# Merged attention and FFN kernel: a mask in two parts, LayerNorm's variance plus epsilon and negated mean on VectorE, and the last two steps in another order

## The chip, the cores and the metric

One NeuronCore of a Trainium2 chip runs the kernel. The metric is device time in microseconds of one execution. Three timed executions of the kernel before took 692.0, 689.85 and 688.17 us (median 689.85). A fourth one was recorded by the hardware profiler and took 687.63 us, of which the instructions span 685.6 us.

Engine names in the profile: PE is TensorE's matmuls, PEld its weight loads, DVE is VectorE, ACT is ScalarE, POOL is GpSimd, SP is SyncE (DMA queues).

## The reference

The input x is 8 x 1024 tokens of D = 256, in float32. An attention block without softmax is followed by two LayerNorms, then comes a gated FFN whose inputs and weights are rounded to a 4-bit grid in blocks of 16, and a third LayerNorm:

```
q, k, v = heads(x@Wq + bq), heads(x@Wk + bk), heads(x@Wv + bv)   # 16 heads of 16
q = elu(q) + 1;  k = elu(k) + 1;  k = k / sqrt(sum(k*k) + 1e-6)
y = x + ((q @ k^T) @ v) @ Wo + bo
y = (y - mean)/sqrt(var + 1e-6) * gamma + beta                 # LN1
x = layernorm(x + y)                                            # LN2, eps 1e-5
fp4(a): per block of 16: scale = max(max|a|/6, 1e-12); grid value nearest a/scale; times scale
h = silu(fp4(x) @ fp4(w_gate)^T) * (fp4(x) @ fp4(w_up)^T)       # inner width 704
out = layernorm(x + fp4(h) @ fp4(w_down)^T)                     # LN3, eps 1e-5
```

## The kernel before, in words

The 8192 tokens are T = 64 tiles of 128 tokens. The program is raw: each engine's instructions are written out in order by hand, and engines wait for each other by counting semaphores. Nothing reorders them. A first phase works through the projections of keys and values; it overlaps with the beginning of a merged loop `step(t)`, t from FIRST = -9 to LAST = T+5 = 69, which is a software pipeline over tiles. From t = 0 on one step does, on each engine and in this order:

- PE: gate and up matmuls of tile t (18, L477 to L479), the transposes of combined tile t+1 (L648), attention of tile t+9 (L618), and the down projection of tile t-4 (17 matmuls, L477 to L479, L670, L671). "Combined tile" n holds the 256 numbers of x of tile n and the 704 of h of tile n-4, 60 blocks of 16 to a token, as 15 lines of 64 numbers. They are quantised together.
- DVE: `residual` (L1129), the rounding mask `cut` of combined tile t+2 (L1098), block maxima of x (L1067), LN1's sum (L1135), statistics (L1157, L1160), the low part of h's codes `low_h` (L1112, which frees the bank into which PE transposes the next tile), the gating (L1121), statistics (L1167), `bn_aggr` of up to three LayerNorms (L1140), the low part of x (`low_x`, L1105, which PE's next gate and up matmuls wait for; in late steps it stands further back), the rest of the gating (L1123), block maxima of h (L1073), and `joint_scales` (L1086, L1088, L1090).
- POOL: `roots(t)`, four instructions on [128 x 3] for the three LayerNorms at once: variance + epsilon (L1287), negated mean (L1288), power -1/2 (L1290), negated mean times root (L1293); then the dequantisation of combined tile t+1 or t+2 (L1333, L1335, or L1324), the division by scales (L1302 for h, L1305 for x), and LN1's affine (L1311, L1315).
- ACT: evictions of transposes to their high parts (L829, L843, L846), silu, the three normalisations (`ln1_apply`, `ln2_apply`, `ln3_apply`, L866 to L880), and conversions in the quantisation (L805, L807, L814).

There are three kinds of steps. For even n from 12 to 54 (`by_dma(n)`, 22 tiles) the transposes of combined tile n are done by DMA rather than PE; the mask then writes 16 lines (1024 numbers, one line is padding) where it writes 15 otherwise (960). From t = 57 on, and before 6, dequantisation comes at another place in POOL's list. For n > 63 the combined tile holds only h (11 lines, 704 numbers). After t = 63 there are no more gate and up matmuls; the remaining steps drain the pipeline.

## Time and profile before

| | before |
| --- | --- |
| timed executions, us | 692.0, 689.85, 688.17 (median 689.85) |
| profiled execution, us | 687.63 |
| its span, us | 685.6 |
| mean granted TensorE clock | 0.997 |
| PE busy, us (share of the span) | 667.9 (97%) |
| PEld busy | 584.8 (85%) |
| POOL busy | 612.0 (89%) |
| DVE busy | 570.2 (83%) |
| ACT busy | 524.4 (76%) |
| chain that ended last | PE 69%, POOL 13%, issue 9%, DMA 3%, DVE 3%, ACT 2% |

The span is the time from the first to the last recorded instruction; 687.63 - 685.6 = 2.03 us of the execution lie around it. Busy times are of one engine and overlap with those of the others. The chain is the work that ended last, followed back from the last instruction; a share there says who was waited for, on an average over all stages.

### The profile page before, as it was taken

To read this page: it belongs to the slowest core of one execution; us is meant where nothing else is said; L and a number is where in the kernel's file an instruction comes from. 1 tells how busy PE (TensorE), PEld (TensorE's weight loads), DVE (VectorE), ACT (ScalarE), POOL (GpSimd) and SP (SyncE) were. 2 spreads that over 40 slices of the span, in tenths; PEclk is the share of its full clock that TensorE was granted. 3 is DMA by queue.
4 is the path that set the end of the run, shared out by engine and by line. 5 is a ranking of instruction groups with operands and counts; after the bars stand their busy time and mean duration, and the time that the engine had idled before them with its cause. 6 is when DMAs were issued, how large, how long until landed. Compare 5 with 4: busy or idle time off the path is not lost.

```text
span 685.6 us, 14440 instructions
## 1 busy us (share of the span) xinstructions
PE 667.9 (97%) x4216; PEld 584.8 (85%) x4216; DVE 570.2 (83%) x1438; ACT 524.4 (76%) x1037; POOL 612.0 (89%) x925
## 2 busy tenths in 40 slices
PE   7999999999999899999999999999999999999995
PEld 6888888888887789888989998999989989999994
DVE  5678778776779888899899999999988899988774
ACT  4677777775778667788888889888898888887663
POOL 3988898998979998898999999999999999998766
PEclk9999999999999999999999999999999999999998
DMA  8543344444311111444757555665557664500001
GB/s 271 193 139 132 120 134 130 139 139 154 124 63 32 34 60 47 95 96 97 143 116 160 129 128 115 124 163 131 126 98 119 112 145 95 110 17 16 32 17 46
DMA packets 51099, 74.39 MB, mean 109 GB/s; under 512 B 26380, under 2 KB 31054, under 8 KB 51022
## 3 DMA queue, kind: packets, MB, share of 16 engines
q1 hardware_dynamic: 50602, 73.35, 42.8%
q8 instruction: 34, 0.56, 0.3%
q14 instruction: 43, 0.35, 0.2%
q10 hardware_dynamic: 420, 0.13, 0.1%
HBM read 41.75 MB, written 25.89 MB: 99 GB/s over the span
## 4 chain that ended last, share of the span: by engine, by line
PE 69%; POOL 13%; issue 9%; DMA 3%; DVE 3%; ACT 2%; SPq 0%; POOLq 0%; DVEq 0%; ACTq 0%
PE banks L477 18%; PE banks L478 17%; PE banks L479 17%; PE banks L618 6%; POOL arena L1335 4%; PE banks L648 3%; POOL arena L1302 3%; PE banks L540 3%; DMA resid<-scales_scratch 2%; PE banks L488 2%; POOL arena L1305 1%; POOL lnbuf L1311 1%; PE banks L501 1%; POOL arena L1324 1%; DMA resid<-in_L_attn_Wv_dram 1%
## 5 line engine op out<-in xcount | busy, mean ns | idle before, releaser
L477 PE MATMUL banks<-wgu_hi,actT_lo 128*128 128x512 f32 (+1 forms) x384 | 145.5, 379 | 0.3 <-DVE actT_lo L1105 0.2
L478 PE MATMUL banks<-wgu_lo,actT_hi 128*128 128x512 f32 (+1 forms) x384 | 143.6, 374 | 0.0
L479 PE MATMUL banks<-wgu_hi,actT_hi 128*128 128x512 f32 (+1 forms) x384 | 143.2, 373 | 0.0
L477 PE MATMUL banks<-wd_hi,actT_lo 128*128 128x256 f32 x320 | 100.3, 313 | 0.1
L1302 POOL TENSOR_TENSOR arena<-arena 128x704 f32<-128x704 f32 x64 | 89.6, 1401 | 10.8 <-DVE arena L1090 10.8
L479 PE MATMUL banks<-wd_hi,actT_hi 128*128 128x256 f32 x320 | 90.3, 282 | 0.0
L478 PE MATMUL banks<-wd_lo,actT_hi 128*128 128x256 f32 x320 | 90.2, 282 | 0.0
L477 PEld LDWEIGHTS banks<-wgu_hi,actT_lo 128*128 128x128 f32 x384 | 72.4, 188 | 11.9 <-DVE actT_lo L1105 1.5
L479 PEld LDWEIGHTS banks<-wgu_hi,actT_hi 128*128 128x128 f32 x384 | 72.1, 188 | 10.5
L478 PEld LDWEIGHTS banks<-wgu_lo,actT_hi 128*128 128x128 f32 x384 | 72.4, 189 | 9.6
L1335 POOL TENSOR_TENSOR arena<-arena,s 128x960 f32<-128x960 f16 (+2 forms) x46 | 75.9, 1649 | 0.0
L807 ACT ACTIVATE arena<-arena 128x960 f16<-128x960 bf16 (+2 forms) x68 | 64.8, 953 | 5.9 <-POOL arena L1305 5.2
L1290 POOL TENSOR_TENSOR rstd<-ve,mhalf 128x3 f32<-128x3 f32 x78 | 68.9, 883 | 0.0
L1112 DVE TENSOR_TENSOR actT_lo<-banks,actT_hi 128x768 fp32r<-128x768 f32 x64 | 60.6, 947 | 9.7 <-ACT actT_hi L846 9.7
L814 ACT ACTIVATE arena<-arena 128x1024 uint16<-128x1024 uint16 (+3 forms) x68 | 66.3, 975 | 2.2
L1260 POOL TENSOR_TENSOR xs<-arena 128x512 f32<-128x512 f32 x48 | 61.0, 1293 | 7.0 <-DMA arena<-in_L_attn_beta_dram 7.0
L618 PE MATMUL banks<-mo,resid 128*128 128x256 f32 x256 | 65.8, 380 | 0.0
L859 ACT ACTIVATE arena<-banks 128x512 f32<-128x512 f32 x64 | 37.8, 591 | 32.4 <-PE banks L479 32.4
L477 PEld LDWEIGHTS banks<-wd_hi,actT_lo 128*128 128x128 f32 x320 | 60.8, 190 | 1.6 <-DVE actT_lo L1112 0.3
L478 PEld LDWEIGHTS banks<-wd_lo,actT_hi 128*128 128x128 f32 x320 | 60.9, 190 | 1.3
L479 PEld LDWEIGHTS banks<-wd_hi,actT_hi 128*128 128x128 f32 x320 | 60.8, 190 | 0.0
L1073 DVE TENSOR_REDUCE arena<-arena 128x44 f32<-128x704 f32 x64 | 56.8, 887 | 2.5
(146 smaller groups left out, 1966.3 us busy)
## 6 DMA issues: line engine op xcount, KB each, us to landing
xs<-x_plus_scratch SPq DMA_DIRECT2D x32, 512.0 KB, 4.2
x_plus_scratch<-xs SPq DMA_DIRECT2D x24, 512.0 KB, 2.9
resid<-scales_scratch SPq DMA_DIRECT2D x22, 512.0 KB
arena<-in_L_attn_x_dram SPq DMA_DIRECT2D x32, 256.0 KB, 3.6
out_dram<-arena SPq DMA_DIRECT2D x32, 256.0 KB, 6.1
x_plus_scratch<-arena SPq DMA_DIRECT2D x4, 512.0 KB, 2.9
x_plus_scratch<-resid SPq DMA_DIRECT2D x4, 512.0 KB, 3.4
resid<-in_L_attn_x_dram SPq DMA_DIRECT2D x4, 256.0 KB, 6.2
```

What stands on the lines that cost most here:

```text
L477: nc.tensor.matmul(dst, sl, mh, start=(k == 0), stop=False, skip_group_check=shared)
L478: nc.tensor.matmul(dst, sh, ml, start=False, stop=False, skip_group_check=shared)
L479: last = nc.tensor.matmul(dst, sh, mh, start=False, stop=(ended and k == n - 1), skip_group_check=shared)
L618: last = nc.tensor.matmul(ps[:, at_bank(u), 0:D], resid[:, u, m * P:(m + 1) * P], mo[:, u // TPB, m, :], start=(m == 0), stop=(m == KT - 1))
L807: nc.scalar.activation(vqb[n % 2][:, a // RW:b // RW, 0:RW].bitcast(F16), lines(halves(vy[:, n % 2, a:b])), ACT.Copy, scale=F16_ONE).then_ ...
L814: nc.scalar.activation(q, q, ACT.Copy, bias=ROUND_HALF).then_inc(half_s, 1)
L1073: nc.vector.tensor_reduce(am[:, n % 2, XR:RN, 0:4], h[:, n % 2, :].rearrange("p (r c e) -> p r c e", c=4, e=BLK), AX.X, ALU.max, apply_abs ...
L1112: nc.vector.tensor_tensor(vT_lo[:, n % 2, XC:VC, :], v_ps[:, XC:VC, :], f32(vT_hi[:, n % 2, XC:VC, :]), ALU.subtract).then_inc(h_lo_s, 1)
L1260: nc.gpsimd.tensor_tensor(to[:, :, kind, :], xin[:, 2 * r:2 * r + 2, :], row[:, :].unsqueeze(1).broadcast_to([P, 2, D]), ALU.add).then_inc ...
L1290: nc.gpsimd.tensor_tensor(rstd[:, s, :], ve[:, :], mhalf[:, :].broadcast_to([P, 3]), ALU.pow).then_inc(pow_s, 1)
L1302: last = nc.gpsimd.tensor_tensor(blocks(vy[:, s, D:VW]), blocks(h[:, s, :]), each(inv[:, s, D // BLK:VB]), ALU.mult)
L1335: nc.gpsimd.tensor_tensor(blocks(va[:, (n + 1) % 2, a:b]), blocks(vqc[n % 2].bitcast(F16)[:, a:b]), each(s14[:, n % 4, a // BLK:b // BLK]) ...
```

## The change

1. `cut(n)`, the rounding mask on DVE: for the 22 tiles that are turned by DMA, the one instruction on 16 lines becomes two, on lines 13 to 15 and 0 to 12 (`SPLIT = 13`).
2. A new DVE function `root_sums(t)` stands behind the last `bn_aggr` of a step and makes variance + epsilon (a tensor_tensor) and the negated mean (a tensor_scalar), both [128 x 3], in buffers of two slots. It does so for t from 2 to LAST; POOL's `roots(t)` then waits for these two and does only the power and the product. For t below 2 POOL still does all four. `roots(70)`, which nothing used, is gone.
3. In the last steps: `cut(66)` moves on DVE from step 64 to step 63, between the maxima of h and `joint_scales(67)`; on POOL `dequantise(66)` moves ahead of `over_scales(67)`; on ACT `ln3_apply` stands behind the eviction of h's high part from t = 64 on.

```diff
+        SPLIT = 13
+        sums_s = sem("sums_by_dve")
+        SUMMED = [*range(2, LAST + 1)]
+        def summed(t):
+            return 2 * len([u for u in SUMMED if u <= t])
...
-                if there(t - 6):
+                if there(t - 6) and t < T:
                     ln3_apply(t - 6, t)
                 if there(t + 1) and not late(t):
                     high_x(t + 1)
                 if there(t + 1 - LAG) and h_with_x(t + 1):
                     high_h(t + 1)
+                if there(t - 6) and t >= T:
+                    ln3_apply(t - 6, t)
...
                 if by_dma(n):
-                    b = VC * P
-                nc.vector.tensor_scalar(lines(vqc[n % 2].bitcast(U16)[:, a:b]), vqb[n % 2][:, a // RW:b // RW, 0:RW],
-                                        ROUND_MASK, None, ALU.bitwise_and).then_inc(round_s, 1)
+                    nc.vector.tensor_scalar(out[:, SPLIT:, :], source[:, SPLIT:VC * P // RW, 0:RW], ROUND_MASK, None,
+                                            ALU.bitwise_and)
+                    b = SPLIT
+                nc.vector.tensor_scalar(out[:, a // RW:b, :], source[:, a // RW:b, 0:RW], ROUND_MASK, None,
+                                        ALU.bitwise_and).then_inc(round_s, 1)
...
+            def root_sums(t):
+                s = t % 2
+                dve.wait_ge(agg_s, aggregated(t - 1))
+                after(dve, root_s, rooted(t - 2))
+                nc.vector.tensor_tensor(ve_dve[:, s, :], mv[:, s, :, 1], eps_v[:, :], ALU.add).then_inc(sums_s, 1)
+                nc.vector.tensor_scalar(nm_dve[:, s, :], mv[:, s, :, 0], -1.0, None, ALU.mult).then_inc(sums_s, 1)
...
-                if joint(t + 2):
+                if joint(t + 2) and t != T:
                     cut(t + 2)
...
+                if t + 1 in SUMMED:
+                    root_sums(t + 1)
                 if there(t + 1) and t >= 0 and not late(t):
                     low_x(t + 1)
...
+                if t + 1 == T:
+                    cut(t + 3)
                 if joint(t + 4) and not pair(t + 33):
                     joint_scales(t + 4)
...
-                nc.gpsimd.tensor_tensor(ve[:, :], mv[:, s, :, 1], eps_v[:, :], ALU.add).then_inc(ve_s, 1)
-                nc.gpsimd.tensor_tensor(nm[:, :], mv[:, s, :, 0], mone[:, :].broadcast_to([P, 3]), ALU.mult).then_inc(nm_s, 1)
-                pool.wait_ge(ve_s, rooted(t))
-                nc.gpsimd.tensor_tensor(rstd[:, s, :], ve[:, :], mhalf[:, :].broadcast_to([P, 3]), ALU.pow).then_inc(pow_s, 1)
+                if t in SUMMED:
+                    pool.wait_ge(sums_s, summed(t))
+                    sums, means = ve_dve[:, s, :], nm_dve[:, s, :]
+                else:
...
+                nc.gpsimd.tensor_tensor(rstd[:, s, :], sums, mhalf[:, :].broadcast_to([P, 3]), ALU.pow).then_inc(pow_s, 1)
...
+                if t == T:
+                    dequantise(t + 2)
                 if joint(t + 3):
                     over_scales(t + 3)
                 if there(t + 7):
                     ln1_affine(t + 7)
-                if joint(t + 2) and not SHIFT <= t < UNSHIFT:
+                if joint(t + 2) and not SHIFT <= t < UNSHIFT and t != T:
                     dequantise(t + 2)
```

How the instructions stand now, first on DVE in an even step whose tile t+2 is turned by DMA, from its first instruction to the second part of the gating. Before (the mask is L1098, the aggregates L1140, the gating's second part L1123):

```order
L1129 TENSOR_TENSOR arena<-banks,resid 128x256
L1098 TENSOR_SCALAR arena<-arena 128x1024
L1067 TENSOR_REDUCE arena<-resid 128x4x4
L1135 TENSOR_TENSOR lnbuf<-banks,xs 128x256
L1157 BN_STATS st<-arena 128x6
L1160 BN_STATS st<-lnbuf 128x6
L1112 TENSOR_TENSOR actT_lo<-banks,actT_hi 128x768
L1121 TENSOR_TENSOR arena<-arena,banks 128x512
L1167 BN_STATS st<-lnbuf 128x6
L1140 BN_AGGR mv<-st 128x2 x3
L1123 TENSOR_TENSOR arena<-arena,banks 128x192
```

The same place after (line numbers are those of the changed kernel: the masks are L1113 and L1116, the new sums L1164 and L1165). The rows between the maxima of x and the first part of the gating are as before and left out by starting a second piece:

```order
L1147 TENSOR_TENSOR arena<-banks,resid 128x256
L1113 TENSOR_SCALAR arena<-arena 128x192
L1116 TENSOR_SCALAR arena<-arena 128x832
L1080 TENSOR_REDUCE arena<-resid 128x4x4
L1153 TENSOR_TENSOR lnbuf<-banks,xs 128x256
L1182 BN_STATS st<-arena 128x6
```

```order
L1139 TENSOR_TENSOR arena<-arena,banks 128x512
L1192 BN_STATS st<-lnbuf 128x6
L1158 BN_AGGR mv<-st 128x2 x3
L1164 TENSOR_TENSOR ve_dve<-mv,eps_v 128x3
L1165 TENSOR_SCALAR nm_dve<-mv 128x3
L1141 TENSOR_TENSOR arena<-arena,banks 128x192
```

The mask has become two instructions, and two instructions on 3 numbers stand between the aggregates and the gating's second part.

Next, DVE from the maxima of h in step 63 to `low_h` in step 64. Before (the scales of tile 67 are L1086 to L1090, the mask of tile 66 is L1098):

```order
L1073 TENSOR_REDUCE arena<-arena 128x11x4
L1086 TENSOR_SCALAR arena<-arena 128x44
L1088 TENSOR_SCALAR s<-arena 128x44
L1090 RECIPROCAL arena<-arena 128x44
L1129 TENSOR_TENSOR arena<-banks,resid 128x256
L1098 TENSOR_SCALAR arena<-arena 128x704
L1157 BN_STATS st<-arena 128x6
L1140 BN_AGGR mv<-st 128x2
L1112 TENSOR_TENSOR actT_lo<-banks,actT_hi 128x768
```

After (the mask is L1116, the scales L1099 to L1103, the sums L1164 and L1165, `low_h` L1130):

```order
L1086 TENSOR_REDUCE arena<-arena 128x11x4
L1116 TENSOR_SCALAR arena<-arena 128x704
L1099 TENSOR_SCALAR arena<-arena 128x44
L1101 TENSOR_SCALAR s<-arena 128x44
L1103 RECIPROCAL arena<-arena 128x44
L1147 TENSOR_TENSOR arena<-banks,resid 128x256
L1182 BN_STATS st<-arena 128x6
L1158 BN_AGGR mv<-st 128x2
L1164 TENSOR_TENSOR ve_dve<-mv,eps_v 128x3
L1165 TENSOR_SCALAR nm_dve<-mv 128x3
L1130 TENSOR_TENSOR actT_lo<-banks,actT_hi 128x768
```

The mask has moved ahead of the scales, and the sums stand ahead of `low_h`.

Last, POOL from step 64 to the roots of step 65. Before (L1302 divides tile 67 by its scales, L1333 and L1335 dequantise tile 66):

```order
L1302 TENSOR_TENSOR arena<-arena 128x704
L1333 TENSOR_TENSOR arena<-arena,s 128x64
L1335 TENSOR_TENSOR arena<-arena,s 128x704
L1287 TENSOR_TENSOR ve<-mv,eps_v 128x3
L1288 TENSOR_TENSOR nm<-mv,mone 128x3
L1290 TENSOR_TENSOR rstd<-ve,mhalf 128x3
L1293 TENSOR_TENSOR nmr<-nm,rstd 128x3
```

After (L1369 and L1371 dequantise tile 66, L1338 divides tile 67, L1327 is the power and L1329 the product):

```order
L1369 TENSOR_TENSOR arena<-arena,s 128x64
L1371 TENSOR_TENSOR arena<-arena,s 128x704
L1338 TENSOR_TENSOR arena<-arena 128x704
L1327 TENSOR_TENSOR rstd<-ve_dve,mhalf 128x3
L1329 TENSOR_TENSOR nmr<-nm_dve,rstd 128x3
```

The dequantisation stands ahead of the division, and two of the four instructions of the roots are gone.

## Rows read from the trace of the kernel before

**Rows 1.** Stretches: span, then each engine's busy us (instructions), PE clock, DMA share, GB/s
```profile
core 0: us, PE busy (x) PEld busy (x) DVE busy (x) ACT busy (x) POOL busy (x), PEclk, DMA share, GB/s
...
208.00:248.00 40.00, 37.19 (x199) 31.28 (x196) 35.29 (x101) 28.83 (x52) 38.20 (x63) 1.00 0.13 40
...
279.00:318.00 39.00, 37.60 (x226) 33.52 (x225) 35.51 (x92) 30.91 (x60) 32.99 (x48) 1.00 0.55 113
318.00:577.00 259.00, 258.78 (x1563) 234.39 (x1563) 237.42 (x655) 222.95 (x431) 248.88 (x341) 1.00 0.61 124
...
664.00:685.60 21.60, 13.20 (x106) 12.42 (x104) 11.13 (x26) 10.04 (x19) 14.56 (x34) 0.92 0.10 37
```

**Rows 2.** Groups by form, POOL: line, out<-in, xcount | busy us, mean ns | idle before
```profile
L1287 POOL TENSOR_TENSOR ve<-mv,eps_v 128x3 f32<-128x3 f32 x78 | 18.3, 235 | 5.9 <-DVE mv L1140 5.6 <-POOL nmr L1293 0.2
L1288 POOL TENSOR_TENSOR nm<-mv,mone 128x3 f32<-128x3 f32 x78 | 15.5, 199 | 0.0
```

**Rows 3.** Groups by form, the masks on DVE
```profile
L1098 DVE TENSOR_SCALAR arena<-arena 128x960 uint16<-128x960 uint16 x38 | 24.4, 642 | 0.2 <-ACT arena L814 0.2
L1098 DVE TENSOR_SCALAR arena<-arena 128x1024 uint16<-128x1024 uint16 x22 | 12.8, 581 | 2.4 <-ACT arena L814 2.4
```

**Rows 4.** Timeline at 294 and 383: start us, us, instruction, [idle before <-releaser]
```profile
294.44 1.79 POOL L1335 TENSOR_TENSOR arena<-arena,s 128x960 f32<-128x960 f16 x1
294.47 2.04 DVE L1098 TENSOR_SCALAR arena<-arena 128x1024 uint16<-128x1024 uint16 x1
298.83 1.07 PE L648 MATMUL banks<-ident,arena 128*128 128x128 f32 x8 [0.94 <-DVE actT_lo L1112]
...
383.05 0.43 DVE L1098 TENSOR_SCALAR arena<-arena 128x1024 uint16<-128x1024 uint16 x1 [0.23 <-ACT arena L814]
```

**Rows 5.** Timeline at 403, a DVE instruction with two SBUF inputs
```profile
402.84 0.75 POOL L1315 TENSOR_TENSOR lnbuf<-lnbuf,xs 128x256 f32<-128x256 f32 x1
403.16 0.97 DVE L1002 TENSOR_TENSOR resid<-resid 128x512 f32<-128x512 f32 x1
```

**Rows 6.** Timeline at 118, two small DVE instructions beside two of POOL's
```profile
118.02 2.54 POOL L1260 TENSOR_TENSOR xs<-arena 128x512 f32<-128x512 f32 x2
118.78 0.55 DVE L942 TENSOR_SCALAR lnbuf<-lnbuf 128x24 f32<-128x24 f32 x1
119.24 0.16 DVE L943 TENSOR_SCALAR lnbuf<-lnbuf 128x24 f32<-128x24 f32 x1
```

**Rows 7.** Timeline, aggregates and what POOL runs, first and last of 36 steps
```profile
321.56 0.30 DVE L1140 BATCH_NORM_AGGREGATE mv<-st 128x2 f32<-128x6 f32 x3
321.90 0.74 POOL L1311 TENSOR_TENSOR lnbuf<-lnbuf,gamma_b 128x256 f32<-128x256 f32 x1
...
573.63 0.30 DVE L1140 BATCH_NORM_AGGREGATE mv<-st 128x2 f32<-128x6 f32 x3
573.97 0.63 POOL L1305 TENSOR_TENSOR arena<-resid,arena 128x256 f32<-128x256 f32 x1
```

**Rows 8.** Timeline at 650, step 61
```profile
649.90 1.79 POOL L1335 TENSOR_TENSOR arena<-arena,s 128x960 f32<-128x960 f16 x1
649.96 0.17 DVE L1140 BATCH_NORM_AGGREGATE mv<-st 128x2 f32<-128x6 f32 x1
650.59 0.42 DVE L1105 TENSOR_TENSOR actT_lo<-banks,actT_hi 128x256 fp32r<-128x256 f32 x1 [0.45 <-ACT actT_hi L829]
```

**Rows 9.** Timeline from 667, steps 64 and 65
```profile
667.42 1.40 POOL L1302 TENSOR_TENSOR arena<-arena 128x704 f32<-128x704 f32 x1 [1.34 <-DVE arena L1090]
667.53 0.51 DVE L1098 TENSOR_SCALAR arena<-arena 128x704 uint16<-128x704 uint16 x1
668.58 0.93 DVE L1112 TENSOR_TENSOR actT_lo<-banks,actT_hi 128x768 fp32r<-128x768 f32 x1
670.34 0.20 POOL L1287 TENSOR_TENSOR ve<-mv,eps_v 128x3 f32<-128x3 f32 x1
670.44 0.88 PE L648 MATMUL banks<-ident,arena 128*128 128x128 f32 x6 [1.32 <-POOL arena L1335]
670.65 0.85 POOL L1290 TENSOR_TENSOR rstd<-ve,mhalf 128x3 f32<-128x3 f32 x1
```

More of the change, by code:

```diff
@@ L93, in build @@
         ve, nm = (sb(n, [P, 3]) for n in ("ve", "nm"))
+        ve_dve, nm_dve = (sb(n, [P, 2, 3]) for n in ("ve_dve", "nm_dve"))
         rstd, nmr = (sb(n, [P, 2, 3]) for n in ("rstd", "nmr"))
@@ L1095, in cut @@
                 after(dve, deq_s, n - 1)
+                source, out = vqb[n % 2], lines(vqc[n % 2].bitcast(U16)[:, 0:VC * P])
+                b = b // RW
                 if by_dma(n):
-                    b = VC * P
-                nc.vector.tensor_scalar(lines(vqc[n % 2].bitcast(U16)[:, a:b]), vqb[n % 2][:, a // RW:b // RW, 0:RW],
-                                        ROUND_MASK, None, ALU.bitwise_and).then_inc(round_s, 1)
+                    nc.vector.tensor_scalar(out[:, SPLIT:, :], source[:, SPLIT:VC * P // RW, 0:RW], ROUND_MASK, None,
[3 more added lines that the diff above has]
+                                        ALU.bitwise_and).then_inc(round_s, 1)
             def low_x(n):
@@ L1278, in roots @@
             def roots(t):
-                if t < FIRST + 2:
+                if t < FIRST + 2 or t > LAST:
                     return
                 s = t % 2
-                pool.wait_ge(agg_s, aggregated(t - 1))
+                if t not in SUMMED:
+                    pool.wait_ge(agg_s, aggregated(t - 1))
                 after(pool, z1_s, min(t + 6, T))
@@ L1286, in roots @@
                 after(pool, root_s, rooted(t - 1))
-                nc.gpsimd.tensor_tensor(ve[:, :], mv[:, s, :, 1], eps_v[:, :], ALU.add).then_inc(ve_s, 1)
-                nc.gpsimd.tensor_tensor(nm[:, :], mv[:, s, :, 0], mone[:, :].broadcast_to([P, 3]), ALU.mult).then_inc(nm_s, 1)
-                pool.wait_ge(ve_s, rooted(t))
-                nc.gpsimd.tensor_tensor(rstd[:, s, :], ve[:, :], mhalf[:, :].broadcast_to([P, 3]), ALU.pow).then_inc(pow_s, 1)
+                if t in SUMMED:
+                    pool.wait_ge(sums_s, summed(t))
+                    sums, means = ve_dve[:, s, :], nm_dve[:, s, :]
+                else:
+                    sums, means = ve[:, :], nm[:, :]
+                    by_pool = rooted(t) - summed(t) // 2
+                    nc.gpsimd.tensor_tensor(sums, mv[:, s, :, 1], eps_v[:, :], ALU.add).then_inc(ve_s, 1)
+                    nc.gpsimd.tensor_tensor(means, mv[:, s, :, 0], mone[:, :].broadcast_to([P, 3]), ALU.mult).then_inc(nm_s, 1)
+                    pool.wait_ge(ve_s, by_pool)
+                    pool.wait_ge(nm_s, by_pool)
+                nc.gpsimd.tensor_tensor(rstd[:, s, :], sums, mhalf[:, :].broadcast_to([P, 3]), ALU.pow).then_inc(pow_s, 1)
                 pool.wait_ge(pow_s, rooted(t))
-                pool.wait_ge(nm_s, rooted(t))
-                nc.gpsimd.tensor_tensor(nmr[:, s, :], nm[:, :], rstd[:, s, :], ALU.mult).then_inc(root_s, 1)
+                nc.gpsimd.tensor_tensor(nmr[:, s, :], means, rstd[:, s, :], ALU.mult).then_inc(root_s, 1)
             def over_scales(n):
```

## The prediction

> **What bounds the kernel now.** I read the table of stretches first, then the groups by form for the instructions that the change touches, then the timelines at the places where one of them stands next to a running POOL instruction. In the table [rows 1] the reader is to compare PE's busy time with the length of the stretch. From 318 to 577 us PE works 258.78 of 259.00 us: 0.22 us is all that any change of DVE or POOL can gain there, over 36 steps. Gaps are left in three other stretches: 2.81 us at 208 to 248 (40.00 - 37.19), 1.40 us at 279 to 318, and 8.40 us in the last 21.60, where the pipeline drains. POOL's share of the page (89%) is therefore no bound by itself. The second thing to see is how little the other engines have in hand beside a full PE: DVE works 237.42 of the 259.00 us, so it idles 21.58 us, 0.60 us a step; POOL idles 10.12 us, 0.28 a step. A change that moves work from POOL to DVE gains nothing while PE is full, and loses once DVE gets over 0.60 us a step.
>
> The third reading is what the two engines do to each other. A DVE instruction with two SBUF inputs that started at 403.16 lasted 0.97 us and ended at 404.13; POOL's L1315 had ended at 403.59, 0.54 before, which leaves 0.54 for the work on its 512 numbers [rows 5]. The mask of 16 lines at 294.47 lasted 2.04 us instead of 0.43: it ended at 296.51, and POOL's L1335, started 0.03 before it, at 296.23 [rows 4]. At 118.78 a small DVE instruction lasted 0.55 us, ending 0.04 after the end of POOL's first L1260 (118.02 + 1.27); the next, at 119.24, took 0.16, though POOL's second L1260 was under way [rows 6]. I read this as: certain DVE instructions wait until POOL's running instruction ends, and one that stands right behind can slip into the same gap.
>
> **The change, part by part.** The sum is made against the profiled execution, 687.63 us (span 685.6, and 2.03 around it).
>
> *POOL's two instructions.* 78 of 235 ns and 78 of 199 ns [rows 2]; pipelined, they take 0.31 us a step (L1287 starts at 670.34, L1290 at 670.65) [rows 9]. 67 to 68 of the 78 steps lose them, some 21 us of POOL's busy time. While PE is full this is worth at most the 0.22 us of idle PE, and I take 0.2.
>
> *Steps 1 to 5, 208 to 248.* POOL saves 0.31 in each of four steps, 1.24 us together. But the new sums stand directly ahead of `low_x`, which PE's next gate and up matmuls wait for, and there the sums' own 0.23 and their wait (both below) come in. The ends are -1.2 (all of POOL's gain arrives at PE) and +1.1 (four waits of 0.28 do). I take 0, the middle.
>
> *The mask in two parts.* 22 instructions took 581 ns on the mean [rows 3]; an undisturbed one took 0.43 [rows 4]. 22 x 0.15 us, 3.3 us, is hence what POOL's running instruction held them up by. Three of them fall on L1335, at steps 10 to 14; the one of 2.04 us is shown, and behind it PE stood 0.94 us for `low_h` [rows 4]. The 15-line form, with an odd count, takes 642 ns, but has no hold-up to speak of in its mean [rows 3]; 11 lines take 0.51 [rows 9]. So 13 lines should take about 0.57, between those two. Three lines have no row; the nearest is a small instruction of 0.16 [rows 6], and I take 0.23 for 192 numbers. With the overlap of neighbours the pair is about 0.73, 0.30 more than an undisturbed 0.43, on every second step: 0.15 us of DVE per step. In return no mask waits for L1335. The gain is PE's idle time at 279 to 318, -1.4, if all of it is due to them; the other end is 0, if the pair is held up as well.
>
> *The new sums.* Two small instructions issue in 0.23 us (the nearest: 0.16 for one [rows 6], less the overlap of the two). Variance + epsilon has two SBUF inputs, so by the reading above it waits for what POOL runs. Step by step over 318 to 577 I compared the end of the last aggregate with POOL's instruction at that time. In the first of the 36 steps the aggregates end at 321.86 and the next POOL instruction starts at 321.90; in the last they end at 573.93 and L1305 starts at 573.97 [rows 7]. Both starts lie 0.04 behind the aggregates, so the sum either just slips ahead or waits out most of 0.63 to 0.74. Over the 36 steps the remaining time of POOL's instruction was 0.10 to 0.67 us, 0.28 on the mean. So a step gets 0.15 (mask) + 0.23 + 0.28 = 0.66 us more on DVE, against 0.60 of idle time. 36 x 0.06 = 2.2 us, of which I take +2.0. The ends: 0 if the sums do not wait (0.38 fits in 0.60), and 36 x 0.66 = 24 us if none of DVE's idle time can be used. Idle time is usable as far as DVE waits in it for PE, and most of it does (`residual` waits for the down projection), so the value near 0 is the better one. What is late next, when it overflows, is `low_h` and with it PE's transposes.
>
> What is queued behind the wait: on DVE the gating's second part, the maxima of h and the scales; for the scales waits POOL's division (L1302). On POOL the power now waits for the sums in place of the aggregates, later by 0.23 to 0.51 a step, against the 0.31 which it saves; that comes out near nothing.
>
> *Step 61.* Here dequantisation stands in another place, and L1335 starts at 649.90, 0.23 before the aggregate ends (649.96 + 0.17). The sums stand still until 651.69. `low_x`, which ran at 650.59 [rows 8], would start at about 651.73: 1.14 us later, in a stretch without slack behind it.
>
> *Steps 64 and 65.* Now L1302 starts at 667.42, L1335 ends at 670.38, and PE, idle for 1.32 us, transposes tile 66 at 670.44 [rows 9]. Moved ahead of L1302's 1.40 us, the dequantisation no longer sets this. Next comes `low_h`, which ended at 669.51 (668.58 + 0.93): 0.93 us are to be had. But L1302 then starts shortly ahead of step 64's sums, and about 0.85 us of it are left when they come. So `low_h` would start at 668.58 + 1.14 (step 61) + 0.85 + 0.23 (the sums) = 670.80 and end at 671.73: PE starts 1.3 later than at 670.44, and with a last 0.1 for the steps behind I take +1.4. The ends: -0.9 if the sums never wait, and +2.8 if they wait for the whole of L1335 and L1302 (1.79 + 1.40 + twice 0.23, less those 0.93, rounded up). That ACT's `ln3_apply` stands further back has its price in these ends.
>
> The sum: 0 - 1.4 (masks) - 0.2 (POOL late) + 2.0 (DVE over its idle time) + 1.4 (end) = +1.8 us, so 687.63 + 1.8 = 689.4 for an execution like the profiled one. The four known times average 689.4 (692.0, 689.85, 688.17, 687.63), 1.8 above the profiled one; with this the forecast is 691.2 us.
>
> **The rivals.**
>
> *A. The sums do not wait for POOL.* For it: POOL's small instructions and DVE's aggregates run side by side in [rows 7] with no hold-up, and three numbers may be too few to conflict. Against it: the small one at 118.78 [rows 6]. Then 0.38 us a step hide in 0.60, step 61 costs nothing, the end gains 0.9, the masks 1.4, POOL 0.2, and of the 1.2 in steps 1 to 5 half arrives: -3.1, so 686.3.
>
> *B. DVE becomes the bound.* The negated mean, on one input, does not slip through behind the sum but waits for POOL's next instruction as well. A step then gets some 0.65 us more (L1305 takes 0.63, L1311 0.74 [rows 7]): 1.31 against 0.60, from 0.60 on everything counts, 36 x 0.71 = 25.6, less 1.6 for masks and POOL, plus 1.4 at the end. That is slower, 714.8; where only every second step is caught, 702. Against it: the second of two small ones did slip through [rows 6]. The Trainium skill, page "Advanced Engine Details and Errata", section "VectorE Performance Modes", speaks for it: an instruction from SBUF to SBUF takes the second port, which it shares with GpSimd so that they block each other, where the major counts of source and destination are both even, or odd, above 1 and equal. Three and three would be such a case, so by that page the negated mean waits by itself. The mask of 16 lines fits the even half of this rule [rows 4]; a mask of 15 lines, odd and equal on both sides, should then be held up too, and its mean of 642 ns shows no such waits [rows 3], so the rows do not bear out the odd half.
>
> *C. Everything hides.* The waits fit into DVE's idle time and the gains are where PE does not wait: no change, 689.4.
>
> **How the numbers follow.** Forecast 0.43, A 0.30, B 0.17, C 0.10. The forecast's own range is 688 to 695 (early steps and masks at their good or bad end, steady steps at +0 to +4). From A I take the upper part, so the range begins at 685.5; B's mild part reaches 698. Less than 1 in 10 is left out on either side. A measurement of this kernel can tell about 0.5% from no change, 3.45 us: faster means under 686.0, slower over 692.9. Faster: two thirds of A and a little of the forecast, 0.22. Slower: B with 0.16 and the upper third of the forecast with 0.15, 0.31. The same: 0.47.
>
> **What would show it.** The sum behind the aggregates lasting 0.1 to 0.7 us and ending with a POOL instruction: right; 0.16 throughout: A. The negated mean above 0.3 us: B. Masks of 13 lines at about 0.57 and none above 1 us at steps 10 to 14; PE gaps at 279 to 318 below 0.5. PE at 258.8 of 259 again in the steady steps would make +2.0 wrong; a longer stretch with PE waiting for `low_h` or `low_x` would bear it out. In step 61 the sums should last 1.4 to 1.8 us. PE's transposes of tile 66 should start near 672, later than before by over 1 us, released by DVE and not by POOL; earlier than 670.44 would make the step on the end wrong.

## The result and the profile after

The changed kernel is slower: 702.38 us (median of 6 runs) against 689.01, a ratio of 1.0191 with a 95% interval of 1.0164 to 1.0218. One of the six runs of the kernel before took 945.59 us; it is in that median and not in the ratio, and the other five have a median of 688.17. The forecast of 691.2 and its range up to 698.0 missed it. The profiled execution took 700.78 us, with a span of 698.7, 13.1 more than before.

PE's work is the same, 4216 matmuls at a mean granted clock of 0.996 (0.997 before), but its busy time rose from 667.9 to 675.5 us. So PE's idle time in the table below shows only part of the delay. DVE's busy time rose from 570.2 to 614.0 us, POOL's fell from 612.0 to 585.9. So DVE took on 43.8 us where POOL gave up 26.1. Where the end came later is read from the table of stretches. Its columns are those of [rows 1]; this is the changed kernel.

```profile
208.00:248.00 40.00, 36.36 (x198) 30.22 (x199) 38.09 (x107) 28.13 (x53) 37.98 (x54) 1.00 0.12 40
279.00:318.00 39.00, 38.93 (x241) 35.32 (x240) 36.44 (x109) 32.65 (x62) 32.43 (x40) 1.00 0.61 112
318.00:577.00 259.00, 256.42 (x1528) 229.78 (x1527) 253.82 (x730) 217.81 (x422) 228.89 (x264) 1.00 0.59 122
577.00:664.00 87.00, 83.88 (x520) 75.64 (x519) 79.85 (x205) 62.84 (x118) 70.31 (x84) 1.00 0.23 53
664.00:698.70 34.70, 24.31 (x164) 22.52 (x162) 25.63 (x63) 16.48 (x31) 17.83 (x25) 0.93 0.08 31
```

The kernel before, in the one of these stretches that [rows 1] leaves out:

```profile
577.00:664.00 87.00, 87.00 (x544) 79.42 (x543) 73.33 (x188) 65.47 (x121) 75.33 (x111) 1.00 0.18 48
```

At 279 to 318 PE is now full (38.93 of 39.00, before 37.60): the masks' part came as forecast. At 318 to 577 DVE works 253.82 of 259.00 us where it worked 237.42 [rows 1], and PE, which had waited 0.22 us, waits 2.58. At 577 to 664, where PE had been busy for the whole 87.00, it waits 3.12.

Time is best followed by when PE begins each step's gate and up matmuls. The changed kernel's beginning less that of before, in us, over the steps: 

```
step     0      6      10     15     50     57     60     63     end
       +1.34  +1.69  +1.64  -0.07  +5.00  +5.31  +8.33  +9.85  +13.12
```

The first 1.34 lie ahead of any changed instruction on the path; in the profiled executions below this number is between -0.4 and +1.5, so I put it down to the execution. From step 10 to 15 the kernel gains 1.7. It loses 5.1 from step 15 to 50, 4.5 from 57 to 63, and 3.3 in the drain.

The groups by form show the loss on DVE (line, tiles, shapes, count, then busy us and mean ns, then idle before). The two sums are L1164 and L1165, the masks' parts L1113 and L1116; [rows 3] has the mask in one.

```profile
L1164 DVE TENSOR_TENSOR ve_dve<-mv,eps_v 128x3 f32<-128x3 f32 x68 | 29.8, 438 | 2.6 <-DVE mv L1158 0.2
L1165 DVE TENSOR_SCALAR nm_dve<-mv 128x3 f32<-128x3 f32 x68 | 23.7, 348 | 0.1
L1116 DVE TENSOR_SCALAR arena<-arena 128x832 uint16<-128x832 uint16 x22 | 12.7, 577 | 0.0
L1113 DVE TENSOR_SCALAR arena<-arena 128x192 uint16<-128x192 uint16 x22 | 5.4, 244 | 1.3 <-ACT arena L824 1.3
```

The masks cost what was forecast (0.577 and 0.244 us, forecast 0.57 and 0.23). Both sums are long: 438 and 348 ns for three numbers, where an undisturbed one takes 0.15 to 0.16. The timeline of DVE shows how. First two steps, at 329 and 373 us (start, duration, instruction); what POOL runs there follows.

```profile
328.72 0.61 DVE L1164 TENSOR_TENSOR ve_dve<-mv,eps_v 128x3 f32<-128x3 f32 x1
329.26 0.15 DVE L1165 TENSOR_SCALAR nm_dve<-mv 128x3 f32<-128x3 f32 x1
...
373.46 0.16 DVE L1164 TENSOR_TENSOR ve_dve<-mv,eps_v 128x3 f32<-128x3 f32 x1
373.54 0.71 DVE L1165 TENSOR_SCALAR nm_dve<-mv 128x3 f32<-128x3 f32 x1
```

```profile
328.59 0.73 POOL L1347 TENSOR_TENSOR lnbuf<-lnbuf,gamma_b 128x256 f32<-128x256 f32 x1
...
372.69 0.73 POOL L1347 TENSOR_TENSOR lnbuf<-lnbuf,gamma_b 128x256 f32<-128x256 f32 x1
373.50 0.73 POOL L1351 TENSOR_TENSOR lnbuf<-lnbuf,xs 128x256 f32<-128x256 f32 x1
374.42 0.86 POOL L1327 TENSOR_TENSOR rstd<-ve_dve,mhalf 128x3 f32<-128x3 f32 x1 [0.19 <-DVE nm_dve L1165]
```

At 328.72 the sum starts 0.13 behind POOL's L1347 and lasts until 329.33, 0.01 past the end of L1347; the mean behind it takes 0.15. At 373.46 POOL's L1347 has just ended (373.42); the sum goes through at once, and the mean, started 0.04 after L1351, lasts to 374.25, 0.02 after L1351's end. POOL's power then has to wait for the mean. So one of the two is held in nearly every step: if the first finds the gap between two POOL instructions, the second does not, and is held for a whole one. Of the 36 steps from 15 to 50 the sum is held in 23, the mean in 12 (in one step both), neither in 2 (held means here: it lasts more than 0.2 us).

In the later steps POOL's instruction is L1371, 1.79 us long. DVE and POOL at step 58 (637 us) of the changed kernel, in that order:

```profile
637.32 0.16 DVE L1164 TENSOR_TENSOR ve_dve<-mv,eps_v 128x3 f32<-128x3 f32 x1
637.40 1.78 DVE L1165 TENSOR_SCALAR nm_dve<-mv 128x3 f32<-128x3 f32 x1
639.10 0.41 DVE L1123 TENSOR_TENSOR actT_lo<-banks,actT_hi 128x256 fp32r<-128x256 f32 x1
```

```profile
637.37 1.79 POOL L1371 TENSOR_TENSOR arena<-arena,s 128x960 f32<-128x960 f16 x1
```

`low_x` (L1123), which PE's next gate and up matmuls need, stands right behind. Step 59 repeats this, and in steps 57, 61, 62 and 63 the sum is held, for 1.79, 1.61, 1.31 and 1.32 us as its duration. Step 61 of [rows 8] and the drain of [rows 9] now read as follows (POOL's dequantisation L1371 and division L1338, DVE's sums and `low_h` L1130, PE's transposes L658, each engine by itself):

```profile
660.18 1.61 DVE L1164 TENSOR_TENSOR ve_dve<-mv,eps_v 128x3 f32<-128x3 f32 x1
661.71 0.15 DVE L1165 TENSOR_SCALAR nm_dve<-mv 128x3 f32<-128x3 f32 x1
661.78 0.41 DVE L1123 TENSOR_TENSOR actT_lo<-banks,actT_hi 128x256 fp32r<-128x256 f32 x1
...
675.25 1.32 DVE L1164 TENSOR_TENSOR ve_dve<-mv,eps_v 128x3 f32<-128x3 f32 x1
...
680.87 1.36 DVE L1165 TENSOR_SCALAR nm_dve<-mv 128x3 f32<-128x3 f32 x1
682.15 0.94 DVE L1130 TENSOR_TENSOR actT_lo<-banks,actT_hi 128x768 fp32r<-128x768 f32 x1
```

```profile
659.98 1.79 POOL L1371 TENSOR_TENSOR arena<-arena,s 128x960 f32<-128x960 f16 x1
...
675.19 1.36 POOL L1371 TENSOR_TENSOR arena<-arena,s 128x704 f32<-128x704 f16 x1
679.50 1.36 POOL L1371 TENSOR_TENSOR arena<-arena,s 128x704 f32<-128x704 f16 x1
680.82 1.40 POOL L1338 TENSOR_TENSOR arena<-arena 128x704 f32<-128x704 f32 x1
```

```profile
672.53 0.81 PE L658 MATMUL banks<-ident,arena 128*128 128x128 f32 x6
677.65 0.85 PE L658 MATMUL banks<-ident,arena 128*128 128x128 f32 x6 [1.21 <-DVE actT_lo L1130]
683.24 1.36 PE L658 MATMUL banks<-ident,arena 128*128 128x128 f32 x6 [2.71 <-DVE actT_lo L1130]
```

The transposes of tile 66 are the last of these rows: at 683.24, released by DVE, where they stood at 670.44, released by POOL [rows 9]. Of these 12.80 us, 9.85 were there when step 63 began.

### The profile page after: what moved, and what is told of

It is laid out like the page before. It is cut to its first block and busy times, and to the rows that moved or that the text cites. A ratio compares the mean times of both kernels' runs of the same rounds, so it can differ in the third digit from the quotient of the medians.

```text
span 698.7 us, 14455 instructions
## 1 busy us (share of the span) xinstructions
PE 675.5 (97%) x4216; PEld 587.9 (84%) x4216; DVE 614.0 (88%) x1596; ACT 523.5 (75%) x1037; POOL 585.9 (84%) x785
## 5 line engine op out<-in xcount | busy, mean ns | idle before, releaser
L487 PE MATMUL banks<-wgu_hi,actT_lo 128*128 128x512 f32 (+1 forms) x384 | 147.0, 383 | 5.5 <-DVE actT_lo L1123 5.3
L1338 POOL TENSOR_TENSOR arena<-arena 128x704 f32<-128x704 f32 x64 | 89.3, 1395 | 18.0 <-DVE arena L1103 14.8
L1371 POOL TENSOR_TENSOR arena<-arena,s 128x960 f32<-128x960 f16 (+2 forms) x46 | 76.5, 1662 | 0.0
L1360 POOL TENSOR_TENSOR arena<-wo_sb,resid 128x1024 f32<-128x1024 f16 x22 | 48.4, 2199 | 30.7 <-DMA wo_sb<-arena 30.7
L1327 POOL TENSOR_TENSOR rstd<-ve_dve,mhalf 128x3 f32<-128x3 f32 x68 | 58.4, 859 | 11.5 <-DVE nm_dve L1165 11.5
L1130 DVE TENSOR_TENSOR actT_lo<-banks,actT_hi 128x768 fp32r<-128x768 f32 x64 | 60.4, 943 | 6.4 <-ACT actT_hi L856 6.4
```

The costliest lines, as they stand in the source:

```text
L487: nc.tensor.matmul(dst, sl, mh, start=(k == 0), stop=False, skip_group_check=shared)
L1130: nc.vector.tensor_tensor(vT_lo[:, n % 2, XC:VC, :], v_ps[:, XC:VC, :], f32(vT_hi[:, n % 2, XC:VC, :]), ALU.subtract).then_inc(h_lo_s, 1)
L1327: nc.gpsimd.tensor_tensor(rstd[:, s, :], sums, mhalf[:, :].broadcast_to([P, 3]), ALU.pow).then_inc(pow_s, 1)
L1338: last = nc.gpsimd.tensor_tensor(blocks(vy[:, s, D:VW]), blocks(h[:, s, :]), each(inv[:, s, D // BLK:VB]), ALU.mult)
L1360: nc.gpsimd.tensor_tensor(v_turned(n)[:, a:VC, :], codes[:, a:VC, :].bitcast(F16), s_each[:, a:VC, :], ALU.mult).then_inc(deq_s, 1)
L1371: nc.gpsimd.tensor_tensor(blocks(va[:, (n + 1) % 2, a:b]), blocks(vqc[n % 2].bitcast(F16)[:, a:b]), each(s14[:, n % 4, a // BLK:b // BLK]) ...
```

## The experiments

The theory after the result (theory 1): each of the two sums, when it starts while POOL works on certain instructions, waits for that instruction's end; one right behind another can use the same gap. Rival 2: the loss comes from the masks or from the last steps' order. Rival 3: it comes from the longer way from aggregates over DVE to POOL's power. All ratios are to the kernel before, run on the same chip beside them: its median was 689.38 beside the first four, 689.13 beside the next four and 688.08 beside the last two.

| kernel | us | ratio (95%) |
| --- | --- | --- |
| all but the sums | 689.60 | 0.9999 (0.9977 to 1.0020) |
| the sums alone | 712.41 | 1.0336 (1.0295 to 1.0377) |
| changed, mean free of POOL | 694.64 | 1.0077 (1.0050 to 1.0105) |
| changed, mean and sum free | 687.39 | 0.9968 (0.9951 to 0.9985) |
| the same, masks in one | 690.81 | 1.0018 (0.9995 to 1.0041) |
| mean and sum free, masks of 15 lines | 688.35 | 0.9991 (0.9975 to 1.0007) |
| changed, mean ahead of sum | 700.73 | 1.0165 (1.0138 to 1.0193) |
| changed, sums for steps 2 to 57 only | 693.76 | 1.0066 (1.0045 to 1.0086) |
| masks in two parts alone | 691.49 | 1.0039 (1.0019 to 1.0060) |
| mean free, two-input sum 3 to 6 | 695.60 | 1.0117 (1.0070 to 1.0164) |

**All but the sums.** The edit to the changed kernel:

```diff
-        SUMMED = [*range(2, LAST + 1)]
+        SUMMED = []
```

> The changed kernel, but POOL makes both sums itself in every step as before; the masks in two parts and the new order of the last steps stay. Theory 1 (the two sums on DVE are held up by POOL's running instruction, one of them in nearly every step): all of the loss goes, and the masks' gain at 279 to 318 us stays: 689.0 - 1.8 = 687, give or take 1.5 for the last steps. Rival 2 (the loss lies in the masks or the last steps): near 700.

689.60: the 12.8 us between this and 702.38 are the sums'. Rival 2 falls. The masks' gain of 2.0 us is there in the profiled execution (step 9 to 15), but it did not stay: 2.3 are lost again between steps 18 and 51, and the median is 2.6 above what I expected. Its row for the steady steps, and two of the waits that PE has there and the kernel before has not:

```profile
318.00:577.00 259.00, 257.16 (x1552) 232.33 (x1551) 237.83 (x668) 221.37 (x429) 245.91 (x339) 1.00 0.60 123
```

```profile
369.84 0.85 PE L658 MATMUL banks<-ident,arena 128*128 128x128 f32 x6 [0.28 <-DVE actT_lo L1130]
399.54 1.10 PE L658 MATMUL banks<-ident,arena 128*128 128x128 f32 x8 [0.73 <-POOL arena L1371]
```

DVE idles 21.17 of the 259.00 us here, nearly as before (21.58), and PE is late all the same. Four waits for `low_h`, in the even steps 22, 28, 34 and 40, make 1.11 us; the one for POOL's dequantisation in step 26 is the largest. The even steps are those with the masks in two parts, but that the added time of the masks causes these waits was not tested by itself.

**The sums alone**, with the old order at the end, and masks of 16 lines again:

```diff
-                    nc.vector.tensor_scalar(out[:, SPLIT:, :], source[:, SPLIT:VC * P // RW, 0:RW], ROUND_MASK, None,
-                                            ALU.bitwise_and)
-                    b = SPLIT
+                    b = VC * P // RW
...
```

(The three dots stand for the old order of the last steps, which the same edit puts back.)

> The kernel before, with nothing but the sums moved to DVE from step 2 on; masks of 16 lines and the old order of the last steps. Theory 1: 702.4 + 1.8 (the masks' gain is missing) and up to 2 either way for the last steps: 702 to 706. Rival 2: near 691.

712.41, worse than expected by 6. The mask in one, L1112 here, takes 1108 ns on the mean where it took 581 [rows 3]:

```profile
L1112 DVE TENSOR_SCALAR arena<-arena 128x1024 uint16<-128x1024 uint16 x22 | 24.4, 1108 | 0.2 <-ACT arena L824 0.2
```

One of them, and the dequantisation that POOL had under way:

```profile
373.78 1.02 DVE L1112 TENSOR_SCALAR arena<-arena 128x1024 uint16<-128x1024 uint16 x1
```

```profile
372.73 1.79 POOL L1365 TENSOR_TENSOR arena<-arena,s 128x960 f32<-128x960 f16 x1
```

The mask ends at 374.80, 0.28 behind the end of POOL's L1365 at 374.52. In the kernel before, 17 of the 22 masks fell beside POOL's power and took 0.41 to 0.43 [rows 4]. So the parts of the change are not additive: the masks in two parts are worth 10 us with the sums (712.41 - 702.38; the drain from step 63 on takes 28.77 us here and 29.09 in the changed kernel, so the old order is not what costs). Without the sums they are worth nothing (ratio 0.9999) or, alone, cost 0.4% (below).

**The mean freed.** The same three numbers, each read twice and written in a row of six:

```diff
-                nc.vector.tensor_scalar(nm_dve[:, s, :], mv[:, s, :, 0], -1.0, None, ALU.mult).then_inc(sums_s, 1)
+                nc.vector.tensor_scalar(nm_dve[:, s, :, :], mv[:, s, :, 0:1].broadcast_to([P, 3, 2]), -1.0, None, ALU.mult).then_inc(sums_s, 1)
...
```

(The three dots stand for the buffer's shape and for POOL reading every second number of it; likewise in the next run.)

> The changed kernel, but the negated mean is made in another form: each of the 3 numbers is read twice (3 x 2, the inner step zero) and 6 are written in a row. Variance + epsilon stays a tensor_tensor. Theory 1, and the Trainium skill's rule (Advanced Engine Details and Errata, VectorE Performance Modes: counts odd and equal, or both even, make the instruction share POOL's port; 3 against 6 is neither): the negated mean takes about 0.17 us in every step, the 18 steps in which it stood 0.6 to 1.8 us get them back, the sum's own waits stay: about 695 (steady steps -3, steps 58 to 60 -3, end -1). If any small DVE instruction is held, whatever its counts: the mean still shows 0.7 in those steps and 702. Rival 3 (no hold-up but the longer way from aggregates over DVE to POOL's power costs the time): 702.

694.64, as theory 1 said. The mean (L1166) is never held (the longest of 68 takes 0.16 us), the sum (L1165) as before:

```profile
L1165 DVE TENSOR_TENSOR ve_dve<-mv,eps_v 128x3 f32<-128x3 f32 x68 | 30.3, 445 | 2.6 <-DVE mv L1159 0.2
L1166 DVE TENSOR_SCALAR nm_dve<-mv 128x6 f32<-128x6 f32 x68 | 10.1, 148 | 0.1
```

Rival 3 can't have these 7.7 us: the way from aggregates over DVE to POOL's power has as many instructions as in the changed kernel. The next run takes the rest from it.

**Mean and sum freed.** Variance + epsilon is made from one input each, in two instructions beside the mean:

```diff
-                nc.vector.tensor_tensor(ve_dve[:, s, :], mv[:, s, :, 1], eps_v[:, :], ALU.add).then_inc(sums_s, 1)
-                nc.vector.tensor_scalar(nm_dve[:, s, :], mv[:, s, :, 0], -1.0, None, ALU.mult).then_inc(sums_s, 1)
+                nc.vector.tensor_scalar(ve_dve[:, s, 0:1], mv[:, s, 0, 1:2], EPS_K, None, ALU.add).then_inc(sums_s, 1)
+                nc.vector.tensor_scalar(ve_dve[:, s, 1:7].rearrange("p (c k) -> p c k", k=2),
+                                        mv[:, s, :, 1:2].broadcast_to([P, 3, 2]), EPS_LN, None, ALU.add).then_inc(sums_s, 1)
+                nc.vector.tensor_scalar(nm_dve[:, s, :, :], mv[:, s, :, 0:1].broadcast_to([P, 3, 2]), -1.0, None, ALU.mult).then_inc(sums_s, 1)
...
```

> As the one with the other form of the mean, and variance + epsilon is also made with one input, in two instructions: one for LN1's number alone, one that reads the three twice (3 x 2) and writes 6. So three small instructions of about 0.16 us on DVE (0.31 a step with their overlap, 0.46 with the masks, against 0.60 of idle time). Theory 1: none of them waits, the steady steps are PE's again, 686 to 688. Rival 3: 700 or more, since the way over DVE is now longer still.

687.39: as expected, and faster than before by 0.3%, the lowest median of the ten. Its three instructions (L1165, L1166, L1168), and POOL at the same time:

```profile
327.77 0.15 DVE L1165 TENSOR_SCALAR ve_dve<-mv 128x1 f32<-128x1 f32 x1
327.84 0.15 DVE L1166 TENSOR_SCALAR ve_dve<-mv 128x6 f32<-128x6 f32 x1
327.91 0.15 DVE L1168 TENSOR_SCALAR nm_dve<-mv 128x6 f32<-128x6 f32 x1
```

```profile
327.78 0.72 POOL L1350 TENSOR_TENSOR lnbuf<-lnbuf,gamma_b 128x256 f32<-128x256 f32 x1
```

All three are through by 328.06 while L1350 runs to 328.50, and none of the 204 in this run takes more than 0.16 us. Three instructions cost less than two that wait: freeing the mean is worth 702.38 - 694.64 = 7.7 us, freeing the sum as well 694.64 - 687.39 = 7.3. Together that is 15.0, more than the 12.8 that the waiting sums cost: with free sums the kernel is 2.2 us below the one in which POOL makes them (689.60), which is what the move is worth when nothing waits.

**The same with masks in one:**

```diff
-                    nc.vector.tensor_scalar(out[:, SPLIT:, :], source[:, SPLIT:VC * P // RW, 0:RW], ROUND_MASK, None,
-                                            ALU.bitwise_and)
-                    b = SPLIT
+                    b = VC * P // RW
```

> The kernel in which no sum waits (687.4 us), with the masks of 16 lines in one instruction again. Theory 1, second part (with POOL's roots shorter, its dequantisation starts earlier and lies on the mask, which it did not before): masks of about 1.1 us on the mean as in the run with sums alone (1.108), 22 x (1.11 - 0.82) = 6 us more than the two parts, so 690 to 696. Rival (masks are held up there only because waiting sums make DVE late): masks near 0.58 on the mean, about 689.

690.81, within the expected time, but not for the reason I gave: the masks take 686 ns on the mean, nearer to the rival's 0.58 than to 1.1.

```profile
L1115 DVE TENSOR_SCALAR arena<-arena 128x1024 uint16<-128x1024 uint16 x22 | 15.1, 686 | 3.5 <-ACT arena L825 3.4
```

Of the 22 masks 5 take over 1 us here, 15 with the waiting sums alone, 3 in the kernel before. POOL's roots are as short here as there, so I put most of the holds there down to DVE being late, not to POOL being early. The masks in two parts are worth 3.4 us here.

**Masks of 15 lines:**

```diff
-                if by_dma(n):
+                if by_dma(n) and n == 12:
```

> The kernel in which no sum waits, and the mask of a tile turned by DMA covers only the 15 lines in use, as in the other steps (the padding line is masked once, for tile 12). One instruction of 0.64 us in place of 0.25 + 0.58 with their overlap, 0.09 less on every second step. If the loss left in the steady steps (1.5 us from step 18 to 51) comes from the mask's added time on DVE: 686.5; if not: 687.4 as before.

688.35, not to be told from 687.39 (the intervals overlap). That the 0.09 us of DVE cause the loss left in the steady steps is not shown, and the profiled executions speak against it: from step 18 to 51 PE's delay grows by 1.8 us here and by 1.5 there.

**The mean ahead of the sum:**

```diff
+                nc.vector.tensor_scalar(nm_dve[:, s, :], mv[:, s, :, 0], -1.0, None, ALU.mult).then_inc(sums_s, 1)
                 nc.vector.tensor_tensor(ve_dve[:, s, :], mv[:, s, :, 1], eps_v[:, :], ALU.add).then_inc(sums_s, 1)
-                nc.vector.tensor_scalar(nm_dve[:, s, :], mv[:, s, :, 0], -1.0, None, ALU.mult).then_inc(sums_s, 1)
```

> The changed kernel with the two sums in the other order, the negated mean ahead of variance + epsilon. Theory 1 (either of the two is held by POOL's instruction, and a small one right behind it slips through the gap): the first has a mean of some 0.4 us, the second 0.35, 700 to 704. If a two-input sum can't slip through a gap: it waits behind the mean's wait in most steps, 0.6 us more in each, 715 or more.

700.73. Now the mean (L1164) takes 471 ns and the sum (L1165) 314:

```profile
L1164 DVE TENSOR_SCALAR nm_dve<-mv 128x3 f32<-128x3 f32 x68 | 32.1, 471 | 2.6 <-DVE mv L1158 0.3
L1165 DVE TENSOR_TENSOR ve_dve<-mv,eps_v 128x3 f32<-128x3 f32 x68 | 21.4, 314 | 0.1
```

Whichever stands first waits for the remainder of POOL's instruction (the mean, in 24 of 36 steps); where it need not, the other mostly waits for a whole one (the sum, in 9). Behind a mean that was held, a two-input sum slips through the gap as well as a one-input one.

**The sums on DVE for steps 2 to 57 alone:**

```diff
-        SUMMED = [*range(2, LAST + 1)]
+        SUMMED = [*range(2, 58)]
```

> The changed kernel, with the sums on DVE for steps 2 to 57 alone; from step 58 on POOL makes them. Theory 1: the waits for the long dequantisation (1.3 to 1.8 us) in steps 57 to 65 go, 4.5 us of PE's delay in steps 58 to 63 and 3.3 in the end: 702.4 - 7.8 = 694.6. If those were only a delay from before that shows late: 700 or more.

693.76, as expected: 8.6 us of the loss come from steps 58 and on, where POOL's instruction is 1.4 to 1.8 us long. In its profiled execution PE's delay of 7.64 at step 58 stays 7.64 at step 63 and is 7.79 at the end.

**The masks in two parts alone**, POOL making the sums and the last steps in the old order:

```diff
-        SUMMED = [*range(2, LAST + 1)]
+        SUMMED = []
...
-                if joint(t + 2) and t != T:
+                if joint(t + 2):
                     cut(t + 2)
...
-                if t + 1 == T:
-                    cut(t + 3)
...
-                if t == T:
-                    dequantise(t + 2)
...
```

> The kernel before with the masks of 22 tiles in two parts and nothing else (roots(70) is dropped too). Beside the run with masks and new order of the last steps (689.6), it tells what that order is worth while POOL makes the sums. My theory: nothing, 689.6 again, and the last 25 us after the last gate and up matmuls begin are as in the kernel before within 0.3. Rival: the new order hides a loss of the masks; then 691 or more.

691.49. That is nearer to the rival than to mine: against the run with the new order the ratios differ by 0.4% (1.0039 and 0.9999), 1.9 us in the medians as they stand, taken on two chips. In the profiled executions the drain from step 63's beginning to the end takes 26.26 us here, 25.69 with the new order, 25.81 before, so that it accounts for 0.1 to 0.6; the rest of the difference between the two profiled executions arose in step 32, where PE waits 1.08 us for POOL's dequantisation and which the order does not touch. What the order is worth by itself stays open within these bounds. What it does is seen at PE's transposes of tiles 65 to 67 (L658) in the run with all but the sums, and of tile 67 (L648) in the kernel before:

```profile
666.61 0.82 PE L658 MATMUL banks<-ident,arena 128*128 128x128 f32 x6
669.97 0.84 PE L658 MATMUL banks<-ident,arena 128*128 128x128 f32 x6 [0.51 <-DVE actT_lo L1130]
674.38 0.87 PE L658 MATMUL banks<-ident,arena 128*128 128x128 f32 x6 [1.54 <-POOL arena L1371]
```

```profile
674.40 0.85 PE L648 MATMUL banks<-ident,arena 128*128 128x128 f32 x6 [1.06 <-DVE actT_lo L1112]
```

The wait ahead of tile 66 falls from 1.32 [rows 9] to 0.51, with DVE in POOL's place. Ahead of tile 67, whose division now stands behind, it rises from 1.06, for DVE, to 1.54, for POOL. So most of the gain is only moved: 2.38 us of wait ahead of the two become 2.05.

**A two-input sum in the form that freed the mean:**

```diff
+                nc.vector.tensor_tensor(ve_dve[:, s, :, :], mv[:, s, :, 1:2].broadcast_to([P, 3, 2]),
+                                        eps_v[:, :].rearrange("p (c k) -> p c k", k=1).broadcast_to([P, 3, 2]),
+                                        ALU.add).then_inc(sums_s, 1)
```

> The run with the other form of the mean (694.6), in which variance + epsilon, still a tensor_tensor with two inputs from SBUF, also reads its 3 numbers twice and writes 6. If two inputs from SBUF are enough to be held by POOL's running instruction, whatever the counts: the sum's mean stays at 0.44 us and the time near 694.6. If the counts alone decide (3 to 3 is held, 3 to 6 not): 0.16 us, and 687.4 as with one-input sums.

695.60, and the sum is held as before:

```profile
L1165 DVE TENSOR_TENSOR ve_dve<-mv,eps_v 128x6 f32<-128x6 f32 x68 | 31.2, 459 | 2.6 <-DVE mv L1159 0.2
```

With two inputs from SBUF neither of the two forms is free; with one input the form decides.

## Why the prediction was wrong, point by point

What bounds the kernel was read rightly: PE. That DVE's 0.60 us of idle time a step are free to use was not. In the changed kernel DVE still idles 5.18 of the 259.00 us in the steady steps, 0.15 a step, while PE falls behind by 5.1; without the sums it idles 21.17 and PE falls behind by 2.2. What counts is which instruction is late in a step, not the idle time that is left on the mean.

The masks' gain (-1.4) was right: 1.7 in the changed kernel, 2.0 without the sums. But without the sums the kernel loses 2.3 again from step 18 to 51, where the prediction let the pair's 0.30 us on every second step vanish in DVE's idle time. Of the three masks that it put down to L1335, the first, of 1.43 us at 279.57, lay on the division L1302 (279.32 to 280.72).

The step that failed is the one on the new sums. It priced their wait by the rest of the POOL instruction that was running when the aggregates ended, 0.28 us on the mean, and let the negated mean slip into the same gap every time. That gap is used by whichever of the two comes at the right moment. In the steps where the sum found it, I counted a wait near nothing; there the mean was held for the whole next instruction. The trace shows 0.23 (sum) and 0.19 (mean) us a step, 0.42 instead of 0.28. With the 0.15 of the masks and the 0.23 of issue that is 0.80 against 0.60, and 36 x 0.20 = 7.2 by the prediction's own way, where 2.0 stood; PE's delay grew by 5.1, of which 2.2 come without the sums too. The 0.28 was also misread: from the end of the last aggregate to the end of POOL's instruction the trace of before has 0.08 to 0.61 us, 0.36 on the mean, which by the same way gives 36 x 0.14 = 5.0. [Rows 7] had it in sight: in its first and last step POOL's next instruction starts 0.04 us behind the aggregates.

Step 61 was right in kind and size: its sum lasts 1.61 us (forecast 1.4 to 1.8). The same failure left out the steps around it. I looked for steps in which L1335 was already running at the aggregates' end, and found one. In steps 58 and 59 it starts just behind the sum and holds the mean for 1.78 and 1.79 us; and the sums of steps 57 and 61 to 63 stood under it as well. Steps 57 to 63 cost 4.5 us, where 1.14 stood.

In the drain I let step 64's sums wait 0.85 us. The held one of them lasted 1.36 (the mean, beside L1338), of step 63's 1.32 and of step 65's 1.05. The drain took 3.3 us more, where 0.3 stood beside step 61's share. Of the 0.93 us to be had from the earlier dequantisation, 0.8 were there without the sums ahead of tile 66, but 0.5 of it went again ahead of tile 67.

Steps 1 to 5, taken as 0, cost 0.35; the kernel without the sums, whose instructions there are those of before, shows 0.43, so that this can't be told from 0.

Rival A was wrong, the sums wait. Rival B, at 0.17, has the right time, 702, in its mild form, and that the mean is held for POOL's next instruction. But in B it waits behind a sum that waits too, and the two were held together in 1 of 36 steps. The time is luck as well: B's mild form has some 12.8 us from the steady steps and 1.4 from the end, where 5.1 and, from step 57 on, 7.8 came. I turned from B because of one pair of instructions at 118 us [rows 6] where the second slips through, and because of an argument on the masks that was false. The prediction said that a mask of 15 lines is odd and equal on both sides. By the operands in the trace it reads 15 lines of 64 (with gaps between them) and writes one run of 960 numbers: 15 against 960, neither both even nor equal. One of 16 lines is 16 against 1024, both even. The Trainium skill's rule (page "Advanced Engine Details and Errata", section "VectorE Performance Modes": major counts of source and destination both even, or odd, above 1 and equal, and the instruction takes the port shared with GpSimd) hence agrees with the masks of before, with the 13 lines that took 577 ns beside POOL, 13 against 832, and with the two forms of the mean: 3 to 3, held to a mean of 348 ns; 3 to 6, 148 ns. For the two-input sum, the Trainium skill's "GPSIMD Engine Reference" (section "Key points": contention with instructions in a 2-port mode or with two SBUF inputs) agrees with the sum held in either form, 438 and 459 ns.

## What to carry to other kernels

A small instruction moved from POOL to DVE is not priced by its length: ask of each one whether POOL's running instruction can hold it, and if so take the length of POOL's next instruction as its price, not only what is left of the present one. Where two such instructions stand in a row, the gap between two POOL instructions lets one of them through, and the other is held. A form that is not held (one input, counts that do not pair) is worth more here than fewer instructions: three free ones ran faster than two that wait. And idle time on the mean is no allowance: PE fell behind by 2.2 us in steady steps in which DVE idled 8% of the time.

## What the runs showed of the hardware that was not expected

A one-input DVE instruction on 3 numbers was held for up to 1.79 us (step 59) by a POOL instruction that had started 0.03 us before it, and writing each number twice, 6 in all, made it free (148 ns on the mean of 68). How far the masks are held depends on how DVE and POOL happen to stand: the same 22 instructions on 16 lines took 581 ns on the mean in the kernel before, 1108 with the waiting sums alone, and 686 with free sums. The hold works the other way too. In the last of these runs a mask starts 0.01 us before POOL's dequantisation; the mask takes its usual 0.42, and the dequantisation 2.05 where it takes 1.79 undisturbed:

```profile
485.90 0.42 DVE L1115 TENSOR_SCALAR arena<-arena 128x1024 uint16<-128x1024 uint16 x1
```

```profile
485.91 2.05 POOL L1372 TENSOR_TENSOR arena<-arena,s 128x960 f32<-128x960 f16 x1
```
